# A graph network on one core: ScalarE makes half of the source one-hots of the count matrix, one cell ahead of its evacuation

## The reference

```python
_s = randint((50000,), 0, 6250); _d = randint((50000,), 0, 6250); _loop = arange(6250)
src = concatenate([_s, _d, _loop]); dst = concatenate([_d, _s, _loop])     # then sorted by dst
msg = x[src]
summed = segment_sum(msg, dst, num_segments=n)
x = _layernorm(x + _L0_gnn_ref(...)); x = _layernorm(x + _L1_gnn_ref(...)); ...
```

## Time and profile before

| | |
|---|---|
| median of three executions | 8647.3 us |
| the profiled execution, and its span | 8667.18 us, 8665.4 us |
| the 343 cells, from PE's first matmul to its last | about 1458 to 2988 us |
| the leftover 7 cells | 2994 to 3063 us |
| in the 343 cells: PE, DVE, ACT, POOL busy | 1036, 1042, 616, 864 of 1530 us |
| fours in the 343 cells | 2856 matmuls of line 796 / 8 = 357 |

### The profile page before, as it was taken

One profiled execution on the slowest core, in us unless ns is written; L12 is line 12 of the kernel. 1 busy time (PEld: TensorE's weight loads), 2 busy tenths in 40 slices (PEclk: granted clock), 3 DMA queues, 4 the chain that ended last, 5 costly groups with the idle time before them and its releaser, 6 DMA issues. The chain is left out here.

```text
span 8665.4 us, 151826 instructions
## 1 busy us (share of the span) xinstructions
PE 6356.4 (73%) x40296; PEld 4385.5 (51%) x40297; DVE 4445.3 (51%) x11924; ACT 2214.7 (26%) x4744; POOL 3409.5 (39%) x3460
## 2 busy tenths in 40 slices
PE   0366612666666579999976777767778599979999
PEld 0255501444444336555546777756667455545555
DVE  6877754666767522222227777767777601121111
ACT  1221201443444310100004555535555200000000
POOL 0777776656566100000007777647777200000000
PEclk6688856888999889999989999989998799989999
DMA  0122201322223346776752222222222266646666
GB/s 16 42 71 69 72 6 38 98 93 86 94 94 98 58 142 172 185 189 164 186 135 55 54 54 54 52 51 54 55 54 54 64 190 191 188 140 188 192 191 181
DMA packets 871731, 903.11 MB, mean 104 GB/s; under 512 B 421539, under 2 KB 820226, under 8 KB 864867
## 3 DMA queue, kind: packets, MB, share of 16 engines
q1 hardware_dynamic: 753541, 637.16, 26.8%
q0 software_dynamic: 109664, 179.92, 9.7%
q10 hardware_dynamic: 8064, 80.29, 2.3%
HBM read 722.84 MB, written 93.87 MB: 94 GB/s over the span
## 5 line engine op out<-in xcount | busy, mean ns | idle before, releaser
L1920 POOL DMA_INDIRECT d_row_ring<-table_att,src_at x1664 | 1583.3, 952 | 657.6 <-issue 489.9
L2463 PE MATMUL psum<-e_a_ring,e_parts 128*128 128x448 bf16 x8232 | 1578.7, 353 | 83.0 <-DVE e_parts L2545 76.4
L2463 PEld LDWEIGHTS psum<-e_a_ring,e_parts 128*128 128x128 bf16 x8232 | 806.5, 98 | 824.4 <-issue 88.4
L777 POOL DMA_INDIRECT b_row_ring<-edge_attr,b_entry x896 | 897.9, 1002 | 593.1 <-SPq L754 352.9
L796 PE MATMUL psum<-b_hot 128*128 x2920 | 666.9, 368 | 612.9 <-DVE b_hot L978 476.0
L354 POOL DMA_INDIRECT listed<-a_record,a_slot_no x832 | 868.4, 1044 | 316.1 <-issue 273.5
L1328 PE MATMUL psum<-c_a_ring,c_parts 128*128 128x448 bf16 x4116 | 816.3, 357 | 48.6 <-DMA c_a_ring<-adjacency 44.0
L1945 PE MATMUL psum<-edges_out,edges_in 128*128 128x120 f32 x4896 | 710.5, 306 | 158.4 <-ACT edges_in L2011 157.6
L796 PEld LDWEIGHTS psum<-b_hot 128*128 x2920 | 289.2, 99 | 964.4 <-issue 840.7
L1945 PEld LDWEIGHTS psum<-edges_out,edges_in 128*128 128x128 f32 x4896 | 658.9, 216 | 203.7 <-issue 203.7
L978 DVE TENSOR_SCALAR b_hot<-b_iota,b_key_dst 128x896 int16 (+1 forms) x1460 | 690.8, 473 | 4.6 <-issue 4.2
(11 more groups left out here) (433 smaller groups left out, 7895.4 us busy)
## 6 DMA issues: line engine op xcount, KB each, us to landing
e_a_ring<-adjacency SPq DMA_DIRECT2D x1372, 224.0 KB, 2.8
c_a_ring<-adjacency SPq DMA_DIRECT2D x686, 224.0 KB, 2.9
adjacency<-b_line ACTq DMA_DIRECT2D x49, 1568.0 KB
a_cum<-edge_attr SPq DMA_DIRECT2D x103, 512.0 KB
d_row_ring<-table_att,src_at POOLq DMA_INDIRECT x1664
b_row_ring<-edge_attr,b_entry POOLq DMA_INDIRECT x896
listed<-a_record,a_slot_no POOLq DMA_INDIRECT x832
e_a_left<-adjacency_left SPq DMA_DIRECT2D x28, 224.0 KB, 3.2
```

Of the source, the lines that this page charges most:

```text
L777: pool.indirect_dma_start(out=row_ring[:, u % 4, g, 0:D], out_offset=None, in_=a["edge_attr_128"], in_offset=bass.IndirectOffsetOnAxis(ap= ...
L1920: pool.indirect_dma_start(out=row_ring[:, u % 4, g, :], out_offset=None, in_=table_att[layer], in_offset=bass.IndirectOffsetOnAxis(ap=src_ ...
L2463: mm = nc.tensor.matmul(psum[:, 2 * (turn % 2) + v, 0:WIN], parts[:, piece, s, :], a_ring[:, s % SEVEN, v * WIN:(v + 1) * WIN], start=(s = ...
```

## The change

The source one-hots of the first two columns of each four are no longer made by DVE but by ACT, as relu(1 - (iota - key_id)^2): two Square activations of 128 x 128, each with the bias of its column (`key_below` = -`key_id`), and one Relu over both, 128 x 256, in place. A wait stands between (the Relu reads what the Squares wrote). ACT does this for a cell's fours before it evacuates the cell before: its order becomes sources of cell 1, copy and clear cell 0, sources of cell 2, copy and clear cell 1, and so on. PE waits for ACT's semaphore `s_src_hot` as well as for DVE's before the first half of each four. ACT needs each cell's first column, count of fours and turn, so it reads `spans_of` (which unpacks three values from each of the seven words) where it read `befores`. The last line is written out of the loop. The leftover part does the same for its cells. The semaphore `s_left_n` makes room and becomes one more count of `s_reach`.

```diff
@@ PE, cell
                             hold(pe, s_hot, turn * 2 + (half + 1), s_held_pe)
+                            if half == 0:
+                                hold(pe, s_src_hot, turn * 2 + 2, s_held_pe)
@@ ACT
-                with act.Fori(0, NT) as s:
-                    for w, then in enumerate(befores(act, s * NWIDE + 1, NWIDE)):
-                        hold(act, s_hot_free, then * 2 + HOT, s_held_act)
-                        nc.scalar.copy(line[...], ps_cell[buffer_of[w]]).then_inc(s_copied, 1)
-                        hold(act, s_copied, s * (2 * NWIDE) + 2 * (w + NWIDE) + 1, s_held_act)
-                        cleared(ps_cell[buffer_of[w]])
+                def source_hots(tile, span):
+                    k0, n, at0 = span
+                    here = iota[:, bass.ds(tile * P, P)]
+                    with act.Fori(0, n) as g:
+                        k = nc.s_assert_within(act.snap(k0 + g * 4), 0, COLS - 4,
+                                               skip_runtime_bounds_check_because="k0 is at most COLS - 4 n")
+                        below = key_below[:, bass.ds(k, 4)]
+                        turn = act.snap(at0 + g)
+                        two = hot[:, bass.ds(turn & 1, 1), 0, :, 0:P].rearrange("p a j f -> p (a j) f")
+                        hold(act, s_hot_free, turn * 2 + 1, s_held_act)
+                        for j in range(2):
+                            apart = nc.scalar.activation(two[:, j, :], here, ACT.Square, bias=below[:, j:j + 1])
+                        apart.then_inc(s_src_hot, 1)
+                        hold(act, s_src_hot, turn * 2 + 1, s_held_act)
+                        nc.scalar.activation(two, two, ACT.Relu, bias=1.0, scale=-1.0).then_inc(s_src_hot, 1)
+
+                def taken(s, w, then):
+                    ...   # the copy and the clearing, as they stood in the loop
+
+                source_hots(0, spans_of(act, 0, 1)[0])
+                with act.Fori(0, NT - 1) as s:
+                    later = spans_of(act, s * NWIDE + 1, NWIDE)
+                    for w in range(NWIDE):
+                        source_hots(s + (w + 1) // NWIDE, later[w])
+                        taken(s, w, later[w][2])
@@ ACT, leftover cells
+                        source_hots(tile, (k0, n, act.snap(at0 + more)))
                         hold(act, s_hot_free, (at0 + n + more) * 2 + HOT, s_held_act)
@@ DVE
+                st.by(V.tensor_scalar(key_below[:], key_id[:], -1.0, None, ALU.mult))
@@ DVE, cell
-                                V.tensor_scalar(four[:, half, j, 0:P], iota[:, bass.ds(tile * P, P)],
-                                                ids[:, c:c + 1], None, ALU.is_equal)
+                                if half == 1:
+                                    V.tensor_scalar(four[:, half, j, 0:P], iota[:, bass.ds(tile * P, P)],
+                                                    ids[:, c:c + 1], None, ALU.is_equal)
```

More of the change, by code:

```diff
@@ L651, in gnn_kernel @@
             key_dst = sbb("key_dst", [P, COLS])
+            key_below = sbb("key_below", [P, COLS])
             reach = sbb("reach", [P, 2, COLS])
@@ L688, in gnn_kernel @@
             s_added = bsem("s_added")
-            s_left_n = bsem("s_left_n")
+            s_src_hot = bsem("s_src_hot")
             s_major = bsem("s_major")
@@ L833, in _ @@
                 cells(NT - 1, 3, NWIDE, befores(pe, (NT - 1) * NWIDE + 3, NWIDE - 2))
-                pe.wait_ge(s_left_n, 1)
+                pe.wait_ge(s_reach, 3)
                 pe.wait_ge(s_copied, 2 * (CELLS + NWIDE))
@@ L858, in _ @@
                 act.wait_ge(s_table, 2)
-                with act.Fori(0, NT) as s:
-                    for w, then in enumerate(befores(act, s * NWIDE + 1, NWIDE)):
-                        hold(act, s_hot_free, then * 2 + HOT, s_held_act)
-                        nc.scalar.copy(line[:, bass.ds(s & 1, 1), w * WIDE:(w + 1) * WIDE].rearrange("p a (v f) -> p (a v) f", v=2),
-                                       ps_cell[buffer_of[w]]).then_inc(s_copied, 1)
-                        hold(act, s_copied, s * (2 * NWIDE) + 2 * (w + NWIDE) + 1, s_held_act)
-                        cleared(ps_cell[buffer_of[w]])
+                def source_hots(tile, span):
[13 more added lines that the diff above has]
+                        nc.scalar.activation(two, two, ACT.Relu, bias=1.0, scale=-1.0).then_inc(s_src_hot, 1)
@@ new lines, in taken @@
+                def taken(s, w, then):
+                    hold(act, s_hot_free, then * 2 + HOT, s_held_act)
+                    parity = bass.ds(s & 1, 1) if not isinstance(s, int) else slice(s & 1, (s & 1) + 1)
+                    nc.scalar.copy(line[:, parity, w * WIDE:(w + 1) * WIDE].rearrange("p a (v f) -> p (a v) f", v=2),
+                                   ps_cell[buffer_of[w]]).then_inc(s_copied, 1)
+                    hold(act, s_copied, s * (2 * NWIDE) + 2 * (w + NWIDE) + 1, s_held_act)
+                    cleared(ps_cell[buffer_of[w]])
@@ L868, in _ @@
                                   line[:, bass.ds(s & 1, 1), :].rearrange("p a f -> p (a f)")).then_inc(s_line_out, 16)
+                later = spans_of(act, (NT - 1) * NWIDE + 1, NWIDE - 1)
+                ended = befores(act, CELLS, 1)
+                for w in range(NWIDE):
+                    if w < NWIDE - 1:
+                        source_hots(NT - 1, later[w])
+                    taken(NT - 1, w, later[w][2] if w < NWIDE - 1 else ended[0])
+                act.wait_ge(s_line_out, (NT - 1) * 16 + 16)
+                act.dma_start(adjacency[NT - 1, :, :], line[:, (NT - 1) & 1, :]).then_inc(s_line_out, 16)
                 act.wait_ge(s_line_out, 16 * NT + 16)
-                act.wait_ge(s_left_n, 1)
+                act.wait_ge(s_reach, 3)
                 lines, windows, more = left_of(act)
@@ L876, in _ @@
                         tile, window = left_at(act, i, j, lines, windows)
-                        _, n = cell_of(act, tile * NWIDE + window)
+                        k0, n = cell_of(act, tile * NWIDE + window)
                         at0 = fours_before(act, tile * NWIDE + window)
+                        source_hots(tile, (k0, n, act.snap(at0 + more)))
                         hold(act, s_hot_free, (at0 + n + more) * 2 + HOT, s_held_act)
@@ L1041, in _ @@
                 st.settle(dve)
-                dve.sem_inc(s_left_n, 1)
+                dve.sem_inc(s_reach, 1)
                 dve.sem_inc(s_left, 1)
```

## The result

The changed kernel takes 8883.1 us, the median of four executions (8876.3 to 8890.8); the kernel before, run beside it, 8647.2 us. The ratio is 1.0273 (95% interval 1.0257 to 1.0289). The profiled execution has a span of 8885.2 us where the kernel before had 8665.4, so the profiles show 219.8 us more, and the medians 235.9.

A forecast was written before the change was run, and what follows sets the result against it. DVE and PE were taken to pace the cells in turns, ACT's serial work becoming the path: 8667.2 + 219 (cells) + 10 (leftover) + 2 = 8898 us profiled, 8878 us on the median; 8 in 10 range 8770 to 9000.

The forecast's parts named there:

- S: Time one four's sources add to ACT (two Squares, a wait, the Relu): 1.53 us, range 1.2 to 1.9.
- ACT's serial work: Per line on ACT: seven copy-and-clear steps 13.1 us, sources 11.2, loop-back 4.9; together 29.2 us, all on the path.
- The wait at the middle two: In the line's middle ACT waits 6.5 us for PE's register loads, `two` and cell 3, with nothing it may do.
- T(1): ACT's copy and clearing of cell 1, 1.87 us; its start is time zero for reckoning the middle wait.
- rival 5: PE cools: idler, more cells run at the colder clock, 2.5 us a line, +123 us, 9001 us; chance 0.05.
- cell 1's wait: Sign in the trace: after each line's end, PE's wait at cell 1 would be about 8 us.
- Rival 3: ACT's loop body outgrows its instruction store, its branch costing +173 us, 9051 us, or half, 8964; chance 0.12.
- Rival 4: Activation tables reloaded at each Square or copy: +914 us, 9780 us; chance 0.02.
- So DVE and PE pace the cells in turns: In the 343 cells before the change, DVE and PE wait for each other by turns; a line takes 31.2 us.
- rival 1: The lead is enough and DVE's relief shows: -2.0 to -2.3 us a line, 8540 us; chance 0.07.
- PE's own additions: In PE's cell loop, one more wait a four, about 0.2 us, hidden inside PE's idle time.
- The formula 27.6 + 5.29 S: Time of a line in us by S: 35.7 against 31.2 before; 33.9 at S of 1.2, 37.7 at 1.9.

The follow-up runs named there:

- experiment 4: Changed kernel with ACT's Squares and Relus going to a spare tile, DVE making all four one-hots, PE not waiting for ACT's sources: 8682.9 us.
- experiment 5: Changed kernel with three cells of lead instead of one, source one-hots in a ring of four tiles: 8768.6 us, ratio 1.0150 to the kernel before.
- experiment 3: Kernel before without DVE's source one-hots of the first two columns, nothing on ACT in their place: 8655.7 us, ratio 1.0008.
- experiment 1: Changed kernel without the Relu and the wait before it, Squares writing to a tile of their own, PE still waiting for ACT: 8731.1 us.
- experiment 2: Changed kernel with one more Relu of 128 x 256, into a tile nobody reads, ahead of each pair of Squares: 8905.3 us.
- experiment 6: Changed kernel, one cell of lead, each line's DMA issued after the next line's first evacuation: 8796.9 us, ratio 1.0184 to the kernel before.
- experiment 7: Six kernels on two slower chips, with more lead, later DMA or a PE wait fewer, against the kernel before beside them: ratios 0.9975 to 1.0141.

## Why the prediction was right

It said 8878 us and the chip 8883. That it is only 5 us off is in part luck: the profiled execution was to take 8898 us and took 8887.0, 4 us over its median, where that of the kernel before lies 20 over. Step by step:

- *S*: 1.53 us predicted, 1.46 measured. The Squares are 0.31 us apart (0.32), the Relu starts 0.51 behind the second (0.66: a shorter way to its addresses than I had set), lasts 0.42 (0.45), and the copy starts 0.55 behind the Relu's start (0.55). The first Square stands 0.93 behind the clearing, where the copy stood at 0.85, which I had at nothing. The Trainium skill's figures ("ScalarE: Activation LUTs", section "What ACT_TABLE_LOAD costs") gave an estimated 1.08 us for the three where my rows gave 1.17. The trace has 0.69 for the two Squares and 0.42 for the Relu, 1.11 together, and is nearer to the skill's.
- *ACT's serial work*: 7 x 1.86 + 7.29 x 1.46 + 5.2 = 28.9 us a line, 29.2 predicted. The loop-back adds 5.2 (8.56 - 3.33), against 4.9.
- *The wait at the middle two*: 6.5 predicted, 9.52 - 3.33 = 6.2 measured. The terms under it, from T(1)'s start (means over the 49 lines, worked out from the starts and ends in the trace): cell 2 ends at 2.7 us, 2.1 was set; PE then idles 3.0 (3.5), the `two` takes 5.4 (5.7), cell 3 takes 1.9 (1.8) and ACT sees it 0.2 later; the whole, in which the parts overlap by a little, is 13.1 for 13.3. So a late cell 2 cancelled a shorter idle time and a shorter `two`, which is luck. Cell 2 is late because it takes 2.6 us and not 1.77. That is rival 5 in part, in another place than it named: the matmuls of cells 1 and 2 of a line are at 525 and 477 ns in the mean (369 and 358 before), behind PE's wait for ACT at cell 1, and cell 3, right behind the `two`, is at 353. What the clock costs in all no run takes apart.
- *The 343 cells*: +219 predicted, +212 measured. *The leftover*: +10 and +10 (66.0 to 76.2 us, first to last matmul), with 3 us more between the cells and it.
- *The order of the work* is the cause: experiment 4 takes away the waiting and leaves the work, and 170 of 212 us go; experiment 5 gives the lead back, and 106 go, with the 208 us of waiting for sources down to 4.
- *ACT busy* 1030 predicted, 1014 measured; *PE idle for ACT* 350 predicted, 293 in the cells. One sign missed: *cell 1's wait* after a line's end was to be 8 us. PE's sequencer stands 127 us for it over 48 lines, 2.6 us each, at most 3.3.
- *Rival 3* didn't come: the branch of ACT's loop, whose body grew to some 200 instructions a pass in the trace, takes what it took, against the earlier trace rows. *Rival 4* neither (its price adds up to 9792 us with the leftover, not 9780), there is one table load as before:

```profile
L888 ACTq COMPARE_BRANCH  x48: 42/58/58, 1487.3 to 3165.6; - x48
```
```profile
L2062 ACT ACT_TABLE_LOAD x1 | 1.3, 1283 | 23.9 <-issue 23.9
```

Three steps failed, and the total hid them.

- *"So DVE and PE pace the cells in turns"* and, with it, DVE's relief of up to 114 us and rival 1's price. DVE paces nothing: in experiment 3 its relief gives no gain at all. The 2.8 us of a cell are PE's own sequencer, which stands only 4.7 us for DVE in the whole stage. I took the names of the releasers in the earlier trace rows for causes, though three cells in a row, from 2437.77 us on, had idle times of 1.16, 1.06 and 1.03 us with ACT, DVE and "issue" for names, which three different causes would hardly give. The step entered my sum nowhere, since ACT's chain was longer than either; had ACT's chain been shorter, I'd have been wrong by 100 us.
- *"PE's own additions: one more wait a four, about 0.2 us, lies inside its idle time"*. In the changed kernel it does, at 3.3 us a cell. But the idle time is the sequencer's work, so there is no cover: as soon as ACT no longer sets the pace, each further instruction is paid for, about 0.1 us a four for the wait (experiment 1) and 0.2 with the ring (experiment 5).
- *The formula 27.6 + 5.29 S.* It fits at S = 1.46 (35.3 for 35.6), and its slope doesn't: 4.1 and 3.6 measured. Towards small S, PE's sequencer floors the step of a cell (2.9 to 3.0 us is the commonest in experiment 1); towards larger, an added instruction lies in the shadow of the waits at the two places where ACT stands anyway (at the line's end of experiment 2 the Squares start 6.37 us behind the clearing, for 6.36). The own range of the forecast, 8790 to 8975, was therefore too wide by a quarter.

A smaller one: the line's end was not wholly "hidden today". Before the change PE's sequencer stood 34 us for cleared buffers, at the 16 boundaries that have no `two`. The sum didn't use it.

## What to carry to other kernels

Idle time of an engine is free only for work that nobody soon waits for. ACT was idle for 60% of this stage, and took 398 us of work for a cost of 43; what cost four times as much was that its new results stood in a queue behind its old duty, the evacuation, so that a lead of three buffers became one. Before work is moved from engine A to engine B, write B's new instruction order, and ask of each result how much of B's queue stands before it and what that queue waits for.

Check whose pace it is before paying for relief: if the idle gap before an operation is the same whichever releaser is named, look at the engine's own sequencer: where it passes its rows without a gap, relief elsewhere buys nothing, and each wait and each computed address has a price of its own.

## What the hardware showed that I had not expected

- PE's sequencer passes its register instructions, waits and weight loads at one each 0.09 us in the mean, so a loop body of 30 of them is a floor of 2.80 us under eight matmuls that take 1.75 (experiment 3); 31 of them take 2.91 (experiment 1) and 33 take 3.09 (experiment 5).
- The record of a semaphore wait on PE is 51 ns long whether PE waits or not: all 1573 of the changed kernel are, though PE stands up to 3.3 us before some of them. The wait is the gap ahead of the record.
- ACT's load of seven words to registers takes 1.55 us, and 4.31 us when it stands right behind a DMA that ACT has issued (experiment 6).
- PE's clock followed the pace: in the 343 cells it was granted 0.90 before, 0.83 in the changed kernel (415 ns a matmul), and 0.90 again with three cells of lead. In the changed kernel cells 1 and 2, behind PE's longest wait for ACT, take 2.8 and 2.6 us, between the 1.74 of a cell at the upper level of 2.4 GHz and the 3.13 of one at the lower, 1.2 GHz. So part of what a chain costs is paid as a slower PE.
- On the two chips of experiment 7 the same kernel takes 11239 and 11312 us. PE's idle time there is for the larger part put to "issue" in most kernels (592 us before line 796 in the kernel with the later DMA, 183 of it before the first cell, where the kernel before has 78.7 in the earlier trace rows), up to 10 us and more at a time. Ratios don't carry from one kind of chip to the other; the microseconds lost did within some 15, in the two kernels that ran on both.
